# Moving loads, row maxima, layernorms and low halves between places of a batch in a fused cross-attention and expert kernel

## The reference, cut to what matters

```
# x (16, 100, 128), ctx (16, 1444, 96), 16 heads
x = x + tanh(g_xattn) * xattn(layernorm(x), ctx)      # cross attention, heads of 64
x = x + tanh(g_ffn)   * ffn(layernorm(x))

xattn: q = x w_q, k = c w_k, v = c w_v (inner 1024); softmax(q k^T / 8) v;  @ w_o + b_o
ffn:   h = rmsnorm(X) * norm1; self attention over 100 tokens, 16 heads of 8; X = X + ctx wo
       h2 = rmsnorm(X) * norm2; router over 8 experts, top 2, softmax of the two
       X + shared swiglu(h2) + sum_e combine_e * swiglu_e(h2)     # 128 -> 256 -> 128
```

## Time and profile before

| | before |
|---|---|
| median of 3 runs | 1334.48 us (1333.23 to 1334.59) |
| profiled execution | 1331.99 us, of which the span is 1330.3 us |
| busy PE / PEld | 1246.8 us (94%) / 910.8 us (68%) |
| busy DVE / ACT / POOL | 969.7 (73%) / 821.9 (62%) / 708.3 us (53%) |
| TensorE's mean granted clock | 0.972 |
| low halves on POOL (line 449) | 144, mean 2058 ns |
| low halves on DVE (line 449) | 240, mean 1045 ns |
| maxima on DVE (line 1310) | 585, mean 652 ns |

### The profile page before, as it was taken

The page is one execution under the profiler, slowest core; times in us unless marked ns, Lnnn a source line. Parts: engine busy times, 40 slices in busy tenths (PEclk is TensorE's granted clock), DMA queues, the critical chain, the costliest instruction groups (busy, mean ns, idle before and its releaser), DMA issues.

```text
span 1330.3 us, 34633 instructions
## 1 busy us (share of the span) xinstructions
PE 1246.8 (94%) x14472; PEld 910.8 (68%) x14472; DVE 969.7 (73%) x1762; ACT 821.9 (62%) x1476; POOL 708.3 (53%) x555
## 2 busy tenths in 40 slices
PE   6689699999999999999999999999999999889998
PEld 4356477777677776767676767777767676567776
DVE  6787486868686868686777777786868686956766
ACT  1336476766666666666666666676766666555664
POOL 3125356565655556465656556555555645544554
PEclk7789899999999999999999999999999999899999
DMA  6201603130303030303122120303030200000000
GB/s 170 65 1 23 176 14 79 14 80 13 80 14 73 14 78 9 78 16 69 25 36 57 30 63 13 80 14 80 14 80 14 63 14 16 13 16 1 8 8 13
DMA packets 122277, 57.27 MB, mean 43 GB/s; under 512 B 108262, under 2 KB 117706, under 8 KB 122122
## 3 DMA queue, kind: packets, MB, share of 16 engines
q1 hardware_dynamic: 122122, 55.07, 18.1%
HBM read 15.38 MB, written 0.82 MB: 12 GB/s over the span
## 4 chain that ended last, share of the span: by engine, by line
PE 72%; DVE 10%; ACT 9%; issue 4%; DMA 3%; POOL 1%; SPq 1%; DVEq 0%; ACTq 0%; POOLq 0%
PE psum L777 18%; PE psum L758 9%; PE psum L759 8%; PE psum L760 8%; PE psum L858 8%; PE psum L793 4%; PE psum L890 3%; PE psum L912 3%; PE psum L903 3%; DVE mx L1310 2%; DVE p_lo L449 2%; PE psum L805 2%; DMA qk_hi<-mrow 2%; ACT p L985 2%; ACT p_hi L986 2%
## 5 line engine op out<-in xcount | busy, mean ns | idle before, releaser
L449 POOL TENSOR_TENSOR p_lo<-p,p_hi 128x768 f16<-128x768 f32 (+1 forms) x144 | 295.8, 2058 | 296.5 <-ACT p_hi L986 182.7
L1310 DVE TENSOR_REDUCE mx<-psum 128x1 f32<-128x512 f32 (+1 forms) x585 | 364.0, 652 | 52.1 <-PE psum L858 45.7
L985 ACT ACTIVATE p<-psum 128x768 f32<-128x768 f32 (+1 forms) x256 | 214.9, 839 | 241.8 <-PE psum L760 235.3
L777 PEld LDWEIGHTS psum<-c_both,p_hi 128*128 128x128 f16 x4992 | 255.3, 98 | 65.6 <-issue 31.4
L777 PE MATMUL psum<-c_both,p_hi 128*128 128x97 f16 (+1 forms) x4992 | 280.5, 208 | 6.5 <-ACT acc_sb L1001 6.3
L758 PE MATMUL psum<-qk_hi,cT_both 97*128 97x384 f16 (+1 forms) x768 | 260.2, 339 | 17.7 <-DMA qk_hi<-mrow 11.0
L449 DVE TENSOR_TENSOR p_lo<-p,p_hi 128x768 f16<-128x768 f32 (+1 forms) x240 | 250.8, 1045 | 11.6 <-ACT p_hi L986 10.0
L759 PE MATMUL psum<-qk_lo,cT_both 96*128 96x384 f16 (+1 forms) x768 | 258.9, 337 | 0.0
L760 PE MATMUL psum<-qk_hi,cT_both 96*128 96x384 f16 (+1 forms) x768 | 256.7, 334 | 0.0
L858 PE MATMUL psum<-cT_both,qk_hi 96*128 96x512 f16 (+1 forms) x585 | 216.8, 371 | 21.0 <-issue 10.5
L990 ACT ACTIVATE p<-psum 128x384 f32<-128x384 f32 (+1 forms) x256 | 130.0, 508 | 143.6 <-PE psum L760 142.8
(11 more groups left out here) (201 smaller groups left out, 2111.5 us busy)
## 6 DMA issues: line engine op xcount, KB each, us to landing
c_both<-c_new SPq DMA_DIRECT2D x16, 768.0 KB, 3.9
ctx_nat<-in_ctx_dram SPq DMA_DIRECT2D x16, 528.0 KB
aT<-a_new SPq DMA_TRANSPOSE x64, 2.9
wg<-in_L_ffn_e_gate_dram SPq DMA_DIRECT2D x1, 1024.0 KB, 5.6
wu<-in_L_ffn_e_up_dram SPq DMA_DIRECT2D x1, 1024.0 KB, 8.1
wd<-in_L_ffn_e_down_dram SPq DMA_DIRECT2D x8, 128.0 KB, 5.8
out_dram<-x SPq DMA_DIRECT2D x4, 200.0 KB
x<-in_x_dram SPq DMA_DIRECT2D x1, 600.0 KB
```

Of the source, the lines that this page charges most:

```text
L449: engine.tensor_tensor(p_lo[0:m, i % 3, 0:w], p32[0:m, i % 3, 0:w], p_hi[0:m, i % 3, 0:w], ALU.subtract).then_inc(lo_made(b, i)[0], 1)
L777: t = mm(psum[:, ACCB + bank, k * (C + 1):k * (C + 1) + wide], p[0:m, i % 3, n * P:(n + 1) * P], c[parity][0:m, j, 0:wide], start=(j == 0 ...
L985: a(to32, src, ACT.Exp, scale=DH ** -0.5)
L1310: v.tensor_reduce(mx[:, rt, part:part + 1], bank[:, 0:w], AX.X, ALU.max)\
```

## The change

Five edits. (1) `LO_POOL` gets units 7, 9 and 11: GpSimd makes 12 of the 24 low halves, units 7 to 12 in a row. (2) "m" goes from unit 22 to 21, and the maxima are spread over units 3 to 20; with the new `LO_POOL` in the rule, unit 4 has 2 instead of 3, unit 8 has 3 instead of 2, unit 10 has 4 instead of 2, unit 12 has 2 instead of 1, and unit 21 none instead of 3. (3) The layernorms of groups 1, 2, 3 in batch 0 move from units 0 to 9 to units 7 to 15, and GpSimd's roots to units 9, 11 and 13. (4) `load_experts` goes behind `turn(0, 1)` in batch 1. (5) `acc_evac` signals after each of its two copies, and TensorE waits for each bank apart.

```diff
-    LO_POOL = (4, 5, 8, 10, 12, 16, 18, 20, 22)
+    LO_POOL = (4, 5, 7, 8, 9, 10, 11, 12, 16, 18, 20, 22)
...
-    share = {i: 0 for i in range(3, 22)}
+    share = {i: 0 for i in range(3, 21)}
...
-    plan[22].append(("m", 0))
+    plan[21].append(("m", 0))
...
     for n in range(1, 4):
-        plan[2 * n - 2].append(("la", n))
-        plan[2 * n - 1].append(("lb", n))
-        plan[2 * n + 2].append(("lc", n))
-        plan[2 * n + 3].append(("x", n))
+        plan[2 * n + 5].append(("la", n))
+        plan[2 * n + 6].append(("lb", n))
+        plan[2 * n + 8].append(("lc", n))
+        plan[2 * n + 9].append(("x", n))
...
             row_of(0, "first", 0)
-            load_experts()
             for r in range((B - 4) // 2):
                 for b, kind, parity in ((r * 2 + 1, "odd", 1), (r * 2 + 2, "even", 0)):
                     ctx_made(b + 1, 1 - parity)
                     turn(b - 1, 1)
+                    if b == 1:
+                        load_experts()
                     turn(b, 0)
                     row_of(b, kind, parity)
...
                 if kind == "first":
                     ctx_lo(1, 1)
-                    token_rstd(1)
-                    token_rstd(2)
-                    token_rstd(3)
...
                 for i in range(UNITS):
+                    if kind == "first" and i in (9, 11, 13):
+                        token_rstd((i - 7) // 2)
...
-                if j == 0 and not (isinstance(b, int) and b == 0 and i == 0):
-                    pe.wait_ge(acc_out, b * 2 + i // CH)
...
                     for n in range(TILES[half]):
                         bank, k = divmod(n, PER_BANK[half])
+                        if j == 0 and k == 0 and p is p_hi and c is c_hi and (b or half):
+                            pe.wait_ge(acc_out, (b * 2 + half - 1) * 2 + bank + 1)
...
                 for bank in range(2):
-                    ins = a(acc_sb[:, t0:t1, :], ...)
-                ins.then_inc(acc_out, 1)
+                    a(acc_sb[:, t0:t1, :], ...).then_inc(acc_out, 1)
```

More of the change, by code:

```diff
@@ L211, in flamingo_kernel @@
     SET_DVE = [f"{n}0" for n in LN_A + LN_B] + ["wqT", "xln0", "Mh0hi", "Mh0", "xhi0", "xlnT0", "tn", "bot", "Mh1lo"] + \
-              [f"{n}{g}" for g, ns in ((1, LN_A), (1, LN_B), (2, LN_A), (2, LN_B), (1, ["xln"]), (3, LN_A), (1, ["xhi"]),
-                                       (3, LN_B), (2, ["xln"]), (2, ["xhi"]), (3, ["xln"]), (3, ["xhi"])) for n in ns] + \
-              ["Nh0", "Nh1", "Nh2", "x1 0", "Nh3", "x1 1", "x1 2", "x1 3"]
+              [f"{n}1" for n in LN_A + LN_B] + [f"{n}2" for n in LN_A] + ["xln1"] + [f"{n}2" for n in LN_B] + \
+              ["Nh0", "xhi1"] + [f"{n}3" for n in LN_A] + ["Nh1", "xln2"] + [f"{n}3" for n in LN_B] + \
+              ["Nh2", "xhi2", "x1 0", "Nh3", "xln3", "x1 1", "xhi3", "x1 2", "x1 3"]
     SET_ACT = ["wkT", "tx", "tf", "Mh1", "wvT"]
@@ L611, in normalise @@
                 hi, lo = (a_new[:, k, 0:n, 0:C] for k in range(2))
-                pool.wait_ge(acc_out, at + 1)
+                pool.wait_ge(acc_out, (at + 1) * 2)
                 g.tensor_tensor(acc_rc[:, 0:n], acc_sb[:, 0:n, C], minus_one[:, 0:n], ALU.pow).then_inc(acc_rcp, 1)
@@ L818, in aux @@
                     if n == 1:
-                        pe.wait_ge(acc_out, B * 2)
+                        pe.wait_ge(acc_out, B * 4)
                     if n == 3 * EU:
@@ L1000, in acc_evac @@
                     t0, t1 = bank * PER_BANK[half], min(TILES[half], (bank + 1) * PER_BANK[half])
-                    ins = a(acc_sb[:, t0:t1, :], psum[:, ACCB + bank, 0:(t1 - t0) * (C + 1)].rearrange(
-                        "p (k c) -> p k c", c=C + 1), ACT.Copy)
-                ins.then_inc(acc_out, 1)
+                    a(acc_sb[:, t0:t1, :], psum[:, ACCB + bank, 0:(t1 - t0) * (C + 1)].rearrange(
+                        "p (k c) -> p k c", c=C + 1), ACT.Copy).then_inc(acc_out, 1)
             def self_exp(free, c, g):
@@ L1375, in _ @@
             hi, lo = (a_new[:, k, 0:n, 0:C] for k in range(2))
-            dve.wait_ge(acc_out, at + 1)
+            dve.wait_ge(acc_out, (at + 1) * 2)
             v.reciprocal(acc_rc[:, 0:n], acc_sb[:, 0:n, C]).then_inc(acc_rcp, 1)
```

## The result

The changed kernel takes 1325.07 us (median of 4 runs, 1323.73 to 1326.11), the kernel before 1334.24 us beside it (4 runs, 1333.23 to 1334.59). The ratio is 0.9925 with a 95% interval of 0.9913 to 0.9938, so 8 to 12 us are gained. Forecast were 1319, in 1310 to 1329. The profiled execution took 1323.73 us with a span of 1322.0.

The account below looks back on a forecast made before the run. TensorE was taken to set the pace, with VectorE the bound in batch 0. The terms -12 - 1 + 0 - 2.5 = -15.5 gave 1316.5 us; the median stands 2.5 higher, so 1319, range 1310 to 1329.

Parts of the forecast that it names:

- Expert loads: Batch 1: issuing the loads after the transposes removes a 9.77 us wait and the slow clock after it, -12 us.
- The wait called "issue": Batch 1, line 858: 9.77 us gap, read as a DMA wait for batch 2's transposed context behind load_experts.
- Rival 2: Stall only moves: loads fill the DMA engines from 144 to 156, 4 to 10 us come back; 1326 us, 10%.
- m in unit 21: Each batch boundary: row DMA sent 2.5 to 3 us earlier, but ScalarE is late next; -0.3 us a batch.
- Sums by bank: Each batch: three of 18 matmuls can start under ScalarE's second copy of the sums, -0.13 us.
- Fewer maxima in unit 4: Steady batch, units 4 and 5: one maximum less on VectorE shortens TensorE's wait from 1.0 to about 0.7 us, -0.3.
- Unit 10 behind kbd: Steady batch, unit 10: third of four maxima needs the bank VectorE frees after kbd; +0.6 us, bounds 0 and 1.2.
- GpSimd's row without a wait: Steady batch, units 7 to 12: GpSimd's six low halves come in time, about 1 us margin at unit 7; 0.
- A steady batch together: Sum of the steady-batch terms, 0.07 us, taken as none, with +-0.5 for each of 14 batches.
- Batch 0: VectorE-bound: low halves and maxima -1.4, spread layernorms +3.3 - 3.3, row 0.3; about -1 us, bounds -5 and +3.
- Last batch: Low halves of units 7, 9 and 11 leave VectorE, for which TensorE waits 3.3 us; -2.5 us.

Follow-up runs that it names:

- e1: Kernel before with only load_experts moved behind turn(0, 1) in batch 1: 1322.06 us, ratio 0.9911 to the kernel before.
- e7: Changed kernel with m moved back from unit 21 to unit 22: span 1328.9 us, a steady batch 69.2 to 69.3 us.
- e8: Changed kernel with ScalarE signalling both banks of sums only after the second copy: a steady batch 69.2 us, span up 4.7 us.
- e4: Changed kernel with two of unit 10's four maxima moved to units 7 and 9: 1317.71 us, ratio 0.9883 to the kernel before.
- e3: Changed kernel, same plan of maxima, but GpSimd makes only the old nine low halves in all batches: 1356.43 us, one run.
- e6: Changed kernel with batch 0's layernorms back in units 0 to 9 and GpSimd's roots back: 1323.12 us, one run; batch 0 81.5 us.
- e9: Changed kernel, but in the last batch VectorE makes all low halves of units 7 to 12: that batch's units 8 to 12 take 18.4 us.
- e10: Changed kernel with two maxima moved out of unit 10 and one out of unit 5, to units 7 and 9: 1312.28 us, ratio 0.9840.
- e2: Changed kernel, but GpSimd makes only the old nine low halves in the last batch: that batch's units 8 to 12 take 19.5 us.

## Why the prediction was right, and where it was not

The time lay in the range and the sign was right, but the gain was 10.4 us in the batches where 15.5 were forecast. By its steps:

- *Expert loads, -12*: -11.76 in the changed kernel, -11.91 alone (e1). The loads went out at 146.4 and not at 144, and no pitch shows it. The wait called "issue" was the transposes behind the expert loads. Right, in mechanism and size. Rival 2 did not occur.
- *m in unit 21, -0.3*: -0.31 (unit 23, and e7). Of 0.5 us of visible wait ScalarE held 0.2. Right; that the row of maxima comes later still in a batch here and there was not in it.
- *Sums by bank, -0.13*: -0.21 (e8). Right, and 0.08 too small.
- *Fewer maxima in unit 4, -0.3 beside the matmul moved*: units 3 to 5 fell by 0.36, of which 0.2 is the matmul. Mis-sized by 0.14 (-0.16 in place of -0.3); what came up in its place was VectorE's low half for unit 2, for which TensorE stands 0.24 us in unit 4.
- *Unit 10 behind kbd, +0.6*: 3.27 - 2.39 = 0.88, of which 0.2 is one more matmul that is now counted there, so 0.67. Right: e4 takes it away and gains 0.7 us a batch.
- *GpSimd's row without a wait, 0*: right in itself. I hadn't seen that it also covers unit 9's low half (e3: without it +1.7 to +3.4 us a batch). That VectorE "isn't what TensorE waits for" there was wrong for this plan.
- *A steady batch together, 0.07*: +0.13, and I set the 14 of them to nothing in the sum: 1.7 of the missing 5.1 us.
- *Batch 0, -1*: -0.35 in the profile; 80.3 and 80.4 us in the two kernels with the old batch 0, 79.3 to 80.8 in the five with the new one. The sign and the bounds are right, the terms are not: they add up to -1.7 and were taken as -1, low halves and maxima stood in them at -1.4, where e6 has +1.1 or more for them and the two small edits, and the spreading at nothing net, where it gave 0.7 to 2.2 us. That the total came out near is luck.
- *Last batch, -2.5*: +0.07. This is the step that failed, and it is 2.6 of the 5.1 us. I took three low halves off VectorE at 0.95 each and counted the 2.1 us wait for unit 9's as gone. That wait is gone, and so is one of 1.74 us for GpSimd's layernorm (unit 8 fell from 3.78 to 2.27). But VectorE's weight and router instructions behind it stood beside GpSimd's row: with three low halves less in the stretch VectorE was busy 19.37 us in place of 17.09, `kbd` started 1.85 us later after unit 8, TensorE waited 2.82 us for it, and unit 11 went from 5.57 to 7.12. Over all kernels units 8 to 12 got 0.2 to 0.9 us longer where 2.5 us were to go; the whole last batch varies by more than that, and no run shows 2.5 us.

The rule of the Trainium skill ("GPSIMD Engine Reference", Key points) that GpSimd contends with VectorE instructions with two SBUF inputs or in a 2-port mode was weighed for batch 0 and not for the last batch. The trace agrees with the part on two inputs: the router's 96 columns took 0.24 us in e9 with no GpSimd instruction beside them and 3.94 beside two. `wg_hi`, a float32 to float16 pass, took 0.61 and 2.00 us; whether it runs in such a mode no run here shows. `kbd`, with an input in psum, has a low half of GpSimd's beside it in all 16 batches of the changed kernel and in 2 of the kernel before, and took 1.81 or 1.82 us in each. (The `kbd` of the earlier trace rows had none beside it, so that row alone was no evidence.)

## What to carry to other kernels

Before moving work to an idle engine, list what runs beside it on the engine that it shares an interface with, in every kind of batch: in the steady ones the neighbours were `kbd` and maxima, which read psum and kept their times, and the move cost nothing; in the last one they were float32 passes over SBUF, and it gave all of it back. A wait that a trace calls "issue" can be a DMA wait, and the queue of the engine that issues that DMA shows it. And a planner's load table places work that no one looked at: the step from a ratio of 0.9925 to 0.9840 (e10, about 11 us) is three maxima in other units.

## What I had not expected of the hardware

- A small instruction on VectorE can take as long as whole ones of GpSimd: 96 columns took 0.24 us alone (e9), and 4.28 (before), 4.16 (e2) and 3.94 us (changed) beside a low half of GpSimd's and its split of the tokens.

- The same setup took 49.8 to 52.9 us in twelve profiled executions. Much of it is one run of 16 float32 matmuls (line 725, 734 in e3). TensorE in order of time, e3 and the changed kernel:

```profile
11.10 1.99 PE L734 MATMUL psum<-wu_lo,wg_lo 64*128 64x96 f32 x16 [0.99 <-ACT wu_lo L1058]
```

```profile
11.45 3.69 PE L725 MATMUL psum<-wu_lo,wg_lo 64*128 64x96 f32 x16 [0.99 <-ACT wu_lo L1049]
```

They took 1.99 us in three executions (before, e3, e9), whose setups are the three shortest (50.4, 49.8, 50.3 us), and 3.69 or 3.70 in the nine others (51.8 to 52.9). The granted clock doesn't tell the two apart: from 11.5 to 14.0 us it is 1.00 in the nine, and 1.00, 0.87 and 0.97 in the three. What does, stays open. Between the two profiled executions of this comparison it counts against the changed kernel, with about 1.6 us.
